# Transformer block on one core: order of the first half batch's weights and rows, and one block for projections and attention

## The reference

```python
mod = (silu(c) @ wmod).reshape(4, 6, 1, -1)
sa, ca, ga, sb, cb, gb = (mod[:, i] for i in range(6))
h = layernorm(x) * (1 + ca) + sa
x = x + ga * attention(h)        # q, k, v projections, rope, causal softmax, Wo; 32 heads of 32, 8 kv heads
h = layernorm(x) * (1 + cb) + sb
x = x + gb * (h @ W.T + bias + lora(h))
```

## Time and profile before

| | |
|---|---|
| median of three runs | 2525.1 us |
| the profiled execution | 2528.81 us, of which the span is 2527.0 us |
| granted TensorE clock, mean | 0.986 |
| TensorE matmul busy | 2446.0 us (97%) |
| VectorE busy | 1698.7 us (67%) |
| GpSimd busy | 1647.7 us (65%) |
| ScalarE busy | 1047.3 us (41%) |

### The profile page before, as it was taken

One profiled execution on the slowest core, in us unless ns is written; L12 is line 12 of the kernel. 1 busy time (PEld: TensorE's weight loads), 2 busy tenths in 40 slices (PEclk: granted clock), 3 DMA queues, 4 the chain that ended last, 5 costly groups with the idle time before them and its releaser, 6 DMA issues. The chain is left out here.

```text
span 2527.0 us, 36895 instructions
## 1 busy us (share of the span) xinstructions
PE 2446.0 (97%) x13652; PEld 1681.3 (67%) x13716; DVE 1698.7 (67%) x2878; ACT 1047.3 (41%) x1873; POOL 1647.7 (65%) x865
## 2 busy tenths in 40 slices
PE   5999999999899999999999999998999999999998
PEld 2788888887555555555555555553688788888886
DVE  3666666777787888887888888783655454555553
ACT  3433333331566666666666666665211111111111
POOL 3543333441698998998989999993754554555543
PEclk8999999999899999999999999999999999999999
DMA  7322333352544236334333325321433333333330
GB/s 285 134 91 110 117 117 117 121 137 89 143 110 127 67 85 165 77 81 118 81 99 78 81 68 148 90 58 52 165 94 104 99 90 109 104 94 95 116 92 25
DMA packets 179728, 267.49 MB, mean 106 GB/s; under 512 B 20509, under 2 KB 113885, under 8 KB 178401
## 3 DMA queue, kind: packets, MB, share of 16 engines
q1 hardware_dynamic: 179552, 265.13, 35.7%
HBM read 183.22 MB, written 80.81 MB: 104 GB/s over the span
## 5 line engine op out<-in xcount | busy, mean ns | idle before, releaser
L1054 POOL TENSOR_TENSOR p_sum<-p_sum,p_ring 128x1024 f32<-128x1024 f32 (+2 forms) x465 | 990.7, 2162 | 92.9 <-PE ctx_ps L1112 70.8
L261 DVE TENSOR_REDUCE neg_max<-scores_q 128x1 f32<-128x512 f32 (+1 forms) x1168 | 713.6, 655 | 146.1 <-PE scores_q L248 103.6
L952 ACT ACTIVATE p_ring<-scores 128x512 f32<-128x512 f32 (+1 forms) x896 | 452.8, 565 | 246.5 <-DVE scores L1005 184.0
L1091 PE MATMUL scores<-q_stack,k_stack 98*128 98x512 f32 (+1 forms) x1216 | 426.4, 427 | 18.7 <-ACT p_ring L952 8.6
L248 PE MATMUL scores_q<-k_stack,q_stack 96*128 96x512 f32 (+1 forms) x1473 | 442.7, 379 | 1.0 <-DVE prefetched L1021 1.0
L616 POOL TENSOR_TENSOR roped_hilo<-roped_hilo 128x512 fp32r<-128x512 f32 x80 | 105.6, 1319 | 346.5 <-ACT roped_hilo L458 346.3
L1091 PEld LDWEIGHTS scores<-q_stack,k_stack 98*128 98x128 f32 x1216 | 197.6, 193 | 180.7 <-ACT p_ring L952 95.9
L248 PEld LDWEIGHTS scores_q<-k_stack,q_stack 96*128 96x128 f32 x1473 | 266.1, 192 | 64.8 <-DVE neg_max L261 28.4
L665 PE MATMUL proj_ps<-h_hi,w_hi 128*128 128x512 f32 x768 | 307.5, 400 | 1.7 <-POOL h_lo L609 1.7
L665 PE MATMUL proj_ps<-h_hi,w_lo 128*128 128x512 f32 x768 | 300.6, 391 | 0.0
L665 PE MATMUL proj_ps<-h_lo,w_hi 128*128 128x512 f32 x768 | 300.3, 391 | 0.0
(11 more groups left out here) (169 smaller groups left out, 3567.2 us busy)
## 6 DMA issues: line engine op xcount, KB each, us to landing
q_stack<-qk_t SPq DMA_DIRECT2D x96, 512.0 KB, 6.9
qk_t<-roped_hilo SPq DMA_DIRECT2D x80, 512.0 KB, 2.8
x_in<-in_L_attn_resid SPq DMA_DIRECT2D x32, 512.0 KB, 6.3
ctx_t<-ctx_raw SPq DMA_DIRECT2D x64, 256.0 KB, 4.9
prefetched<-in_L_wmod SPq DMA_DIRECT2D x4, 4096.0 KB, 13.5
prefetched<-ctx_t SPq DMA_DIRECT2D x31, 512.0 KB, 4.1
prefetched<-inv_t SPq DMA_DIRECT2D x124, 128.0 KB, 5.5
k_stack<-qk_t SPq DMA_DIRECT2D x96, 128.0 KB, 8.8
```

What stands on the lines that cost most here:

```text
L261: nc.vector.tensor_reduce(sh.negm[:, lo // HALF, hs[0]:hs[-1] + 1, i:i + 1], src, AX.X, ALU.max, negate=True).then_inc(sh.s_mx.sem, 1)
L952: nc.scalar.activation(p[:, a * per:(a + 1) * per, :], src[:, a * per:(a + 1) * per, :], ACT.Exp, scale=SM_SCALE).then_inc(s_ex.sem, 1)
L1054: nc.gpsimd.tensor_tensor(a, a, probs(n, u), ALU.add).then_inc(s_ap.sem, 1)
L1091: last = nc.tensor.matmul(o[a], ks[n % QS][0:KS, j * P:(j + 1) * P], qs[n % QS][0:KS, h0:h0 + per, lo:lo + w], start=True, stop=True)
```

## The change

Three things change. (1) In the first half batch the splits of weight chunks 2 and 3 come behind all eight row pieces on ScalarE and GpSimd, and chunk c + 4 (not c + 6) is split in step c, up to c = 7; SyncE no longer issues `load_w(6)` to `load_w(11)` ahead of the first store, but one at the end of each of the steps 0 to 5. (2) `project(0, 0)` and `project(0, 1)` become `project_first_two`: piece by piece, both chunks, with `turn_h(0, k + 2)` between them. (3) `qkv` and `attention` write into one block; semaphores take the place of the meeting of the engines.

```diff
-            for c in range(6, NC):
-                load_w(c)
             for m in range(HB):
                 for c in range(NC):
...
                     if c and CHUNKS[c - 1][0] != "v":
                         store_qk(m, c - 1)
+                    if m == 0 and c + 6 < NC:
+                        load_w(c + 6)
@@ scalar (and gpsimd alike, with h_lo and w_lo)
             for k in range(DC):
                 h_hi(0, k)
-                if k % 2:
-                    w_hi(2 + k // 2)
+            for c in range(2, 4):
+                w_hi(c)
...
-                    if m == 0 and c < NC - 6:
-                        w_hi(c + 6)
+                    if m == 0 and c < NC - 4:
+                        w_hi(c + 4)
@@ tensor
+            def project_first_two():
+                pe.wait_ge(s_wl.sem, s_wl.at(2))
+                for k in range(DC):
+                    if k + TPS < DC:
+                        turn_h(0, k + TPS)
+                    pe.wait_ge(s_hl.sem, s_hl.at(k + 1))
+                    for c in range(2):
+                        for n, (a, i) in enumerate(((0, 0), (0, 1), (1, 0))):
+                            last = nc.tensor.matmul(pps[c][:, :], w[a][c][:, k, :], h[0][i][:, k, :],
+                                                    start=(k == 0 and n == 0), stop=(k == DC - 1 and n == 2))
+                        if k == DC - 1:
+                            last.then_inc(s_pj.sem, 1)
...
-            for k in range(TPS, DC):
-                turn_h(0, k)
             for m in range(HB):
                 for c in range(NC):
-                    project(m, c)
+                    if m or c > 1:
+                        project(m, c)
+                    elif c == 0:
+                        project_first_two()
@@ attention: vector
-            nc.vector.memset(ones[:, :], 1.0).then_inc(init.sem, 1)
+            dve.wait_ge(sh.s_pj.sem, sh.s_pj.at(NC * HB))
+            nc.vector.memset(ones[:, :], 1.0).then_inc(s_one.sem, 1)
@@ attention: gpsimd
-            nc.gpsimd.memset(ks[2][MHI:MHI + DH, :].bitcast(F32), 1.0).then_inc(init.sem, 1)
+            pool.wait_ge(sh.s_pj.sem, sh.s_pj.at(NC * HB))
+            pool.wait_ge(sh.s_rl.sem, sh.s_rl.at(NRP * HB))
+            nc.gpsimd.memset(ks[2][MHI:MHI + DH, :].bitcast(F32), 1.0).then_inc(s_k2.sem, 1)
+            pool.wait_ge(s_k2.sem, s_k2.at(1))
@@ attention: tensor
-            pe.wait_ge(init.sem, 2)
+            pe.wait_ge(sh.s_pe.sem, sh.s_pe.at(NC * HB))
+            pe.wait_ge(sh.s_mx.sem, sh.s_mx.at(len(FIRST_MAXIMA)))
...
+                if (n, u) == (2, 0):
+                    pe.wait_ge(s_k2.sem, s_k2.at(1))
...
+                if (n, hf) == (0, 0):
+                    pe.wait_ge(s_one.sem, s_one.at(1))
@@ build
+            block = both.enter_context(nc.Block())
```

More of the change, by code:

```diff
@@ L214, in __init__ @@
         self.init = count("max_init")
+        self.s_pj, self.s_pe, self.s_rl = count("projected"), count("proj_taken"), count("rope_lo")
 def fetch_stack(sp, sh, qs, ks, qk_in, n):
@@ L277, in max_split, with qkv @@
                                 ).then_inc(sh.s_ml.sem, 1)
-def qkv(nc, early, sh, consts, x_in, wq_in, wk_in, wv_in, c_in, wmod_in, silu_cols, mod_cols, rope_in, qk_out, v_out):
+def qkv(nc, block, early, sh, consts, x_in, wq_in, wk_in, wv_in, c_in, wmod_in, silu_cols, mod_cols, rope_in, qk_out, v_out):
     x_t = x_in.rearrange("b (t p) d -> (b t) p d", p=P)
@@ L325, in qkv @@
         s_wh, s_wl = count("w_hi_ready"), count("w_lo_ready")
-        s_pj, s_pe = count("projected"), count("proj_taken")
-        s_rc, s_sh, s_rm, s_rp, s_rh, s_rl = (count(n) for n in (
-            "cos_done", "rot_ready", "sin_done", "roped", "rope_hi", "rope_lo"))
+        s_pj, s_pe, s_rl = sh.s_pj, sh.s_pe, sh.s_rl
+        s_rc, s_sh, s_rm, s_rp, s_rh = (count(n) for n in (
+            "cos_done", "rot_ready", "sin_done", "roped", "rope_hi"))
         s_vt, s_vc = count("v_turned"), count("v_taken")
@@ L622, in _ @@
                 h_lo(0, k)
-                if k % 2:
-                    w_lo(2 + k // 2)
+            for c in range(2, 4):
+                w_lo(c)
             for m in range(HB):
@@ L634, in _ @@
                         rope_lo(m, c - 1)
-                    if m == 0 and c < NC - 6:
-                        w_lo(c + 6)
+                    if m == 0 and c < NC - 4:
+                        w_lo(c + 4)
                     if m + 1 < HB:
@@ L722, in _, with attention @@
                             turn_h(m + 1, k)
-def attention(nc, sh, consts, qk_in, v_in, wmod_in, silu_cols, mod_cols, modv, pre, cs, wo_in, la_in, lb_in, lw_in, s_pre, ctx_out, sums_out, inv_t):
+def attention(nc, block, sh, consts, qk_in, v_in, wmod_in, silu_cols, mod_cols, modv, pre, cs, wo_in, la_in, lb_in, lw_in, s_pre, ctx_out, sums_out, inv_t):
     with ExitStack() as ctx:
@@ L753, in count @@
             return Count(nc, ctx, name, step)
-        init = count("a_init")
+        s_one, s_k2 = count("ones_ready"), count("k_stack2_ready")
         s_st, s_v, s_mr = sh.s_st, sh.s_v, sh.s_mr
@@ L765, in attention @@
         s_fc, s_fh, s_cf = count("first_ctx_scaled"), count("first_ctx_hi"), count("coef_ready")
-        block = ctx.enter_context(nc.Block())
         def ring_place(g, u):
@@ L1583, in build @@
             sh = Shared(nc, both)
-            qkv(nc, early, sh, consts, x, wq, wk, wv, c, wmod, silu_cols, mod_cols, rope, qk_t, v_t)
-            attention(nc, sh, consts, qk_t, v_t, wmod, silu_cols, mod_cols, modv, pre, cs, wo, la, lb, lw, s_pre, ctx_t, sums_t, inv_t)
+            block = both.enter_context(nc.Block())
+            qkv(nc, block, early, sh, consts, x, wq, wk, wv, c, wmod, silu_cols, mod_cols, rope, qk_t, v_t)
+            attention(nc, block, sh, consts, qk_t, v_t, wmod, silu_cols, mod_cols, modv, pre, cs, wo, la, lb, lw, s_pre, ctx_t, sums_t, inv_t)
         linear_half(nc, consts, x, pre, cs, s_pre, w, bias, modv, mod_cols, ctx_t, sums_t, inv_t, out)
```

1 line of the change is left out of this document (removed).

## The result

Eight runs of each kernel: 2516.43 us with the change, 2526.01 us without; ratio 0.9962 with a 95% interval of 0.9953 to 0.9972. That is 9.6 us less, against 11.5 forecast. The profiled execution took 2518.16 us, its span 2516.4 (before 2527.0).

The account below looks back on a forecast made before the run. TensorE was taken to bound the kernel, so time gained early passes to the end. First half batch 5.5 plus seam 6.0 gives 11.5 us: 2525.1 to 2513.6 us, own range 2510 to 2517 (chance 0.62), with rivals 2507 to 2520.

Parts of the forecast that it names:

- Projection 2 at 60.0: First half batch: projection 2 starts at 60.0 behind chunk 2's split, against 64.5, so 4.5 us early.
- Late rows: First half batch: half batch 1's row loads issued at about 62.8, standard deviation at about 77.8 against 75.65 before.
- The two idles: First half batch: TensorE idles 2.1 us before the second v turn and 2.4 us before half batch 1's turns.
- a sign of being wrong: Whole forecast: wrong if, among other signs, the shift at 600 us is under 2 or over 8 us.
- The v store: First half batch: v chunk's store issued at about 79.5, landed by 84; ScalarE's 5.58 us stall shrinks to under 1.
- The seam: Between projections and attention: first mask 4.9 us early, first `values` 6.2 us early; taken as 6.0 us, bounds 3.5 and 8.
- From there VectorE sets the pace: Seam, from the first mask at 636.4: VectorE needs 1.8 us a unit, sixth mask at 644.8.
- rival (c): Seam: TensorE stays at 1.2 GHz through attention's group 0, net 16 us slower, 2541 us; chance 0.04.
- (a): First half batch: half batch 1's late rows take back the early start, 6 us in all, 2519.1 us; chance 0.12.
- (b): Seam: TensorE keeps 2.4 GHz, 7.6 us there and 7 at the start, 14.6 in all, 2510.5 us; chance 0.15.
- (d): Seam: merged block brings nothing, only the first half batch counts, 5.5 us, 2519.6 us; chance 0.07.
- The table load: Seam, ScalarE: load takes 1.28 us, exponentials from 638.2; the skill's drain would cost at most 0.7 us.

Follow-up runs that it names:

- experiment 12: The changed kernel unedited, run once more: 2516.32 us, ratio 0.9960 to the kernel before.
- Experiment 3: The changed kernel with half batch 1's row loads issued ahead of weight chunk 4's load, not behind chunk 5's: 2513.99 us, ratio 0.9962 to the kernel before.
- experiment 1: The changed kernel's first half batch, but projections and attention in two blocks as before: 2518.13 us, ratio 0.9970 to the kernel before.
- Experiment 8: The kernel before with only the first two projections taken together and one block, all loads ahead of the first store: 2523.70 us, ratio 0.9993.
- Experiments 7: The changed kernel with 20 and 4 spare matmuls at the seam, results thrown away: 2511.52 us, ratio 0.9948 to the kernel before.
- 11: Kernel 9 with 10 and 6 spare matmuls at the seam, results thrown away: 2519.42 us, ratio 0.9965 to the kernel before.
- experiment 2: The kernel before with only the seam changed (one block for projections and attention), first half batch as before: 2523.12 us, ratio 0.9988.
- experiment 4: The changed kernel with weight splits in their old places (between row pieces, chunk c + 6 in step c), loads still spread: 2531.76 us, ratio 1.0026.
- 9: The changed kernel with chunks 2 to 5 split between row pieces, chunk c + 4 in steps 2 to 7: 2509.98 us, ratio 0.9947 to the kernel before.
- 5: The changed kernel with the first two projections one after the other again: 2512.35 us, ratio 0.9944 to the kernel before.
- 10: Kernel 9 with the first two projections one after the other: 2518.09 us, ratio 0.9958 to the kernel before.
- Experiment 13: Kernel 11 with eight spare transposes at the head of TensorE's stream, shifting its code: 2502.33 us, ratio 0.9903 to the kernel before.

## Why the prediction was right, and where it was off

**Projection 2 at 60.0.** Measured 59.94, by the step named (chunk 2's rest behind piece 7), with the slow clock that I had assumed for the first pieces; 56.26 in experiment 12, where the clock stayed up. That second case I had not counted.

**Late rows.** `load_x(1)` forecast at 62.8, measured 63.14; standard deviation 77.8, measured 79.07. The second tile landed only in time for moments at 70.39, so the first moments ended 0.7 us late. The rotation behind them was 0.5 us shorter than counted. What the sum left out is one more instruction of VectorE between the last moments and the standard deviation, which took 1.56 us before too:

```profile
77.53 1.50 DVE L514 TENSOR_SCALAR std<-mean_var 128x4 f32<-128x4 f32 x1
```

So the step's mechanism was right and its size 1.3 us too small. Experiment 3 shows that the idle came from it.

**The two idles.** Forecast 2.1 and 2.4 us at full clock; measured one of 3.32, and then 1.2 GHz until 86, which hid the second: projection 5 took from 81.12 to 89. The end of the normalisations came as forecast, at 87.65 for 87.6; the slow clock made TensorE 1.4 us late for it. The first half batch gave 4.9 us in this execution and 9.1 in experiment 12's, with 5.5 forecast: the fall of the clock around the second v turn, which I had held for a bound (1.8 us), came in both, and the clock in the row pieces (2.8 us between the two) decides most of which end it is. The central value was hit by two errors against each other (2.5 us more in the turn and projection 5 at the slow clock, and no second idle of 2.4), not by its working. The 9.1 lie over the 8 that I had named as a sign of being wrong: what I had not counted is a row-piece stage at full clock throughout. In experiment 1, the same first half batch once more, there were two idles, of 1.5 and 3.6 us.

**The v store.** Forecast issued at 79.5, measured 80.27, and ScalarE no longer stalls for it (5.58 us before). Experiment 8, with the loads ahead again, brings the idle back as 6.7 us of TensorE.

**The seam.** TensorE forecast idle some 4 us in pieces, measured 0.83 + 2.02 + 0.83; first mask 4.9 us nearer, measured 5.1 (9.97 in all less 4.9 from before); the sixth mask 8.4 us behind the first, measured 9.2. The failed step is "From there VectorE sets the pace": TensorE at 1.2 GHz sets it, full from 634 to 642. The rows could have told it, since rival (c) itself says that TensorE was full and slow there before. The term was 6.0 and is 4.6: the 5.1 of the first mask less 0.4 that are lost again on the way to the first `values`. Experiments 7 and 11 show what is missing: with the clock kept it is 5.6 and 6.5.

**The rivals.** (a) was partly there: the rows cost 2.3 us or somewhat more, but did not eat the start. (b) the full seam needs the clock that spare work gives; even then it is 6.5 and not 7.6. (c) the clock was back at 643, so no slow group 0. (d) is refuted by the seam in experiment 2's trace (14.31 us against 18.95); its whole time, 0 to 6.1 us less, would not do it alone.

**The table load.** The load stands at 632.08, directly behind the rope part that ends at 632.06, and the exponential starts at 633.37: 1.28 us and no drain beside it. The Trainium skill (ScalarE: Activation LUTs, What ACT_TABLE_LOAD costs) adds a drain of about 1.38 us to every switch of sets. This trace shows none, and the measurement decides.

## What to carry to other kernels

When loads are moved behind stores on an in-order queue, count two steps between a load and its first reader on every engine in the ring; one step too few costs more than the whole change brings (experiment 4 against 9: 20.7 us before the seam). When a stage is pulled forward, list what its old end used to release, and issue those loads by hand: four DMAs two lines up took away the idle that the edit had made. And cut traces at fixed events before believing a total of this size: stretches whose code is untouched can differ by 20 us.

## What the runs showed of the hardware that I had not expected

The linear half, one loop of the same instructions in every kernel, took 759.0, 759.1, 766.6 to 772.6 and 779.0 us; what changed was only the instructions ahead of it (24, 24, 0 and 16 more matmuls on TensorE, in this order). With 24 more, 12 instruction packets moved from 1790 to 2480 us and not 29 or 30, and the waits without a releaser where a pass of the loop begins were gone. The three kernels with one block and serial first projections (2, 5 and 10), in which TensorE has one wait more ahead of the loop, took 772.0 to 772.6 us; all the others without spare work took 766.6 to 769.3. Experiment 13 was made to test the place of the code and hit the time and the packets that it named. That instructions are fetched anew at each pass fits these rows, but no run shows the fetch itself; why 16 more are worse than none with as many packets (29) stays open, and other numbers were not tried.

TensorE idle for 2.0 to 3.3 us with little work around it ran at 1.2 GHz when it came back or within about 1 us of it (80 and 632 us, and 77 us in experiment 12), and stayed there for 3 to 10 us of full work. Idles of 1.0 and 1.2 us in experiment 3 left the clock at 2.4 GHz. And the same kernel ran its row pieces at 1.2 GHz until 49 us in one execution and at 2.4 GHz throughout in another.
